# A recommendation tower: twelve bf16-split tables become sixteen float32r-split ones, and the pairs go over DRAM

## The reference

```python
e = jnp.stack([tbl_0[ids[:, 0]], ..., tbl_31[ids[:, 31]]], axis=1)   # 512 x 32 x 128
dot = jnp.einsum('bnd,bmd->bnm', e, e)
iu, ju = jnp.triu_indices(32, k=1)
z = dot[:, iu, ju]                                                  # 512 x 496
h = jnp.concatenate([z, dense_ctx], axis=1)                         # 512 x 512
h = jnp.maximum(h @ W_top1 + b_top1, 0.0)                           # 512 x 512
h = jnp.maximum(h @ W_top2 + b_top2, 0.0)                           # 512 x 256
y = h @ W_top3                                                      # 512 x 1
```

## Time and profile before

| What | us |
|---|---|
| median of 3 runs (lowest to highest) | 162.18 (161.59 to 163.24) |
| the profiled execution, time of the run | 162.2 |
| its span, first to last instruction | 160.4 |
| TensorE busy / VectorE / ScalarE / GpSimd | 135.5 / 86.9 / 51.4 / 80.5 |
| first pick matmul / last table copied / end of the last copy of y | 10.08 / 81.1 / 158.8 |

### The profile page before, as it was taken

The page is one execution under the profiler, slowest core; times in us unless marked ns, Lnnn a source line. Parts: engine busy times, 40 slices in busy tenths (PEclk is TensorE's granted clock), DMA queues, the critical chain, the costliest instruction groups (busy, mean ns, idle before and its releaser), DMA issues.

```text
span 160.4 us, 2998 instructions
## 1 busy us (share of the span) xinstructions
PE 135.5 (84%) x1216; PEld 94.7 (59%) x1222; DVE 86.9 (54%) x218; ACT 51.4 (32%) x124; POOL 80.5 (50%) x88
## 2 busy tenths in 40 slices
PE   0049999999999999999979999799868977647994
PEld 0013454555454455545378998699658966527992
DVE  0299999998898889277029505402741043352010
ACT  3130322440442144123049932001652025462001
POOL 4777777777778777777734773772600000000000
PEclk9999999999999999999999999999999999685699
DMA  3992367646754774989310210220100000000000
GB/s 75 338 356 53 79 235 246 212 115 215 247 145 153 243 223 104 248 315 367 108 48 22 53 49 18 64 54 16 49 20 0 4 0 0 4 0 0 0 0 1
DMA packets 7023, 17.97 MB, mean 112 GB/s; under 512 B 1873, under 2 KB 2513, under 8 KB 6866
## 3 DMA queue, kind: packets, MB, share of 16 engines
q1 hardware_dynamic: 4450, 12.54, 23.5%
q0 software_dynamic: 2560, 5.25, 12.8%
HBM read 17.78 MB, written 0.00 MB: 111 GB/s over the span
## 4 chain that ended last, share of the span: by engine, by line
PE 78%; DVE 9%; ACT 7%; DMA 3%; issue 2%; SPq 1%; DVEq 0%
PE pick_ps L360 41%; PE pick_ps L394 16%; PE dot_ps L382 10%; ACT feat L267 5%; DVE feat L138 4%; DMA table<-picked 3%; PE turn_ps L369 3%; DVE h L208 3%; PE dot_ps L394 2%; PE turn_ps L394 2%; ACT emb L267 1%; PE pick_ps L406 1%; PE pick_ps L433 1%; DVE rest L191 1%; DVE low L194 1%
## 5 line engine op out<-in xcount | busy, mean ns | idle before, releaser
L179 POOL DMA_INDIRECT rows<-tables,row_no x80 | 79.6, 996 | 34.3 <-issue 23.2
L360 PE MATMUL pick_ps<-onehot,table 128*128 128x512 bf16 x97 | 37.7, 389 | 10.2 <-DVE onehot L204 10.1
L360 PE MATMUL pick_ps<-onehot,rest 128*128 128x512 bf16 x96 | 37.4, 390 | 0.1
L360 PE MATMUL pick_ps<-onehot,low 128*128 128x512 bf16 x95 | 36.9, 388 | 0.1
L204 DVE TENSOR_SCALAR onehot<-pick_id,own_row 128x512 bf16<-128x512 f16 x98 | 31.5, 382 | 2.3 <-PE pick_ps L360 2.0
L138 DVE COPY feat<-dot_ps 16x128 f32<-16x128 f32 (+3 forms) x72 | 19.9, 276 | 19.9 <-PE dot_ps L382 19.0
L394 PE MATMUL pick_ps<-feat,w_sb 128*128 128x128 f32 x208 | 26.0, 288 | 4.0 <-ACT feat L267 4.0
L267 ACT ACTIVATE emb<-pick_ps 128x512 f32<-128x512 f32 x12 | 12.9, 1076 | 49.1 <-PE pick_ps L360 49.1
L394 PEld LDWEIGHTS pick_ps<-feat,w_sb 128*128 128x128 f32 x208 | 25.1, 202 | 4.6 <-ACT feat L267 4.3
L360 PEld LDWEIGHTS pick_ps<-onehot,table 128*128 128x128 bf16 x98 | 9.8, 100 | 21.1 <-issue 10.6
L267 ACT ACTIVATE feat<-dot_ps 16x128 f32<-16x128 f32 (+3 forms) x72 | 18.3, 254 | 10.9 <-PE dot_ps L382 10.2
(11 more groups left out here) (32 smaller groups left out, 41.0 us busy)
## 6 DMA issues: line engine op xcount, KB each, us to landing
table<-picked SPq DMA_DIRECT2D x11, 512.0 KB, 3.6
pick_id_sb<-pick_ids SPq DMA_DIRECT2D x12, 256.0 KB, 4.1
w_sb<-w SPq DMA_DIRECT2D x1, 2048.0 KB
rows<-tables,row_no POOLq DMA_INDIRECT x80, 2.8
table<-picked SPq DMA_DIRECT2D x1, 640.0 KB, 7.4
w_sb<-w SPq DMA_DIRECT2D x1, 512.0 KB
feat<-context SPq DMA_DIRECT2D x1, 256.0 KB, 8.5
id_sb<-row_ids SPq DMA_DIRECT2D x1, 80.0 KB, 1.9
```

What stands on the lines that cost most here:

```text
L179: pool.indirect_dma_start(rows[:, k % ROWS_HELD, i, :], None, tables, bass.IndirectOffsetOnAxis(ap=row_no[:, c:c + 1], axis=0)).then_inc(r ...
L360: last = pe.matmul(out, part[:, at, D * k:D * (k + 1)], onehot[:, c % HOT, :], start=(k == 0 and m == 0), stop=(k == KR[t] - 1 and m == le ...
```

## The change

Numbers first: sixteen tables are picked (eleven of 8 chunks, five of 10: 138 chunks), sixteen gathered (64 gathers, 16 turns; twelve turns stand between picks and four between groups of dots). Row buffers are eight.

A picked table has two parts, both of type float32r. ScalarE copies the table into `high` (`split_high`), VectorE subtracts it from the table into `low` (`split_low`), and TensorE makes two matmuls a chunk. The one-hots are float32r too, compared from 16-bit integer ids that are loaded so. The last one-hot of every table is made by ScalarE in two activations, absolute difference and then 1 minus it (`make_last_onehot`). The first table is loaded in four pieces.

The 32 x 32 products are copied to `dot_sb`, four copies a group and engine, and SyncE stores a block of 128 samples to DRAM in four stores, waits, and loads it back in four loads with the row length taken as 33. So partition a gets, for 16 steps k, the product of features a and a+k+1 (modulo 32, shifted by a row where it wraps): each of the 496 pairs once, and the context, which had been stored behind them. W_top1 then has its own 512 rows. `layer1` is 16 matmuls of 256 columns, and there are two halves of 256 samples in place of four blocks. The layers stand behind all dots and turns. The weights are loaded behind the tables and the context, as before, W_top1 in two loads of 512 KB.

```diff
-PICK = 12
+PICK = 16
...
-TABLES_HELD, IDS_HELD, HOT, ROWS_HELD = 3, 4, 12, 6
+TABLES_HELD, IDS_HELD, HOT, ROWS_HELD = 3, 4, 12, 8
+TURN_WITH = [1, 3, 4, 6, 7, 9, 10, 11, 12, 13, 14, 15]
...
+            for r in range(BLOCKS):
+                sp.wait_ge(dots_act, 2 * r + 2)
+                sp.wait_ge(dots_dve, 2 * r + 2)
+                for s in range(4):
+                    sp.dma_start(dot_out[r][s, 0:F * F, :].rearrange("(a j) g -> a (j g)", j=F),
+                                 dot_sb[32 * s:32 * s + 32, r % 2, :, :].rearrange("p j g -> p (j g)")
+                                 ).then_inc(dots_stored[r], 16)
+                sp.wait_ge(dots_stored[r], 64)
+                skewed = dot_out[r].rearrange("s (a x) g -> a s x g", x=F + 1)
+                for q in range(4):
+                    sp.dma_start(pairs[32 * q:32 * q + 32, r, :, :, :].rearrange("a s c g -> a s (c g)"),
+                                 skewed[:, :, 1 + PC * q:1 + PC * (q + 1), :].rearrange("a s c g -> a s (c g)")
+                                 ).then_inc(pairs_in[r], 16)
...
-                dve.tensor_tensor(rest[:, at, 0:n], table[:, at, 0:n], table_hi[:, at, 0:n],
-                                  ALU.subtract).then_inc(rest_ready, 1)
-                dve.wait_ge(rest_ready, t + 1)
-                dve.tensor_tensor(low[:, at, 0:n], rest[:, at, 0:n], rest_hi[:, at, 0:n],
-                                  ALU.subtract).then_inc(low_ready, 1)
+                dve.tensor_tensor(low[:, at, a:b], table[:, at, a:b], high[:, at, a:b],
+                                  ALU.subtract).then_inc(low_ready, 1)
...
+            def make_last_onehot(t):
+                i, k, c = STEPS.index(KR[t]), KR[t] - 1, CHUNK0[t + 1] - 1
+                act.wait_ge(pick_ids_in[t], 16)
...
+                act.activation(away[:, :], pick_id[:, t % IDS_HELD, :], ACT.Abs,
+                               bias=less_row[:, i, k:k + 1]).then_inc(away_ready, 1)
+                act.wait_ge(away_ready, t + 1)
...
+                act.activation(onehot[:, c % HOT, :], away[:, :], ACT.Relu, bias=1.0, scale=-1.0
+                               ).then_inc(last_onehot_ready, 1)
...
             for t in range(PICK):
                 pick_out(t)
+                if t + 1 < PICK:
+                    make_last_onehot(t + 1)
+                if t in TURN_WITH:
+                    emb_out(TURN_WITH.index(t))
                 if t + 3 < PICK:
-                    ids_out(t + 3)
+                    split_high(t + 3)
...
+                    pe.matmul(out, high[:, at, D * k:D * (k + 1)], onehot[:, c % HOT, :],
+                              start=(k == 0), stop=False)
+                    pe.matmul(out, low[:, at, D * k:D * (k + 1)], onehot[:, c % HOT, :],
+                              start=False, stop=(k == KR[t] - 1)).then_inc(picked_done, 1)
...
-            def layer1(r):
-                pe.wait_ge(feat_act, 2 * r + 2)
-                pe.wait_ge(feat_dve, 2 * r + 2)
+            def layer1(v):
+                pe.wait_ge(pairs_in[2 * v], 64)
+                pe.wait_ge(pairs_in[2 * v + 1], 64)
                 for n in range(N1):
...
+                    for c in range(PC):
+                        last = pe.matmul(h1_ps[v][n], w1_sb[:, c, n * P:(n + 1) * P],
+                                         pairs[:, 2 * v:2 * v + 2, :, c, :],
+                                         start=(c == 0), stop=(c == PC - 1))
```

More of the change, by code:

```diff
@@ L36, in build @@
 def build(nc, row_ids, pick_ids, tables, picked, context, w1, w2, small, y):
-    f32, bf16, i32 = mybir.dt.float32, mybir.dt.bfloat16, mybir.dt.int32
-    f16 = mybir.dt.float16
+    f32, f32r, i32, i16 = mybir.dt.float32, mybir.dt.float32r, mybir.dt.int32, mybir.dt.int16
     ALU = mybir.AluOpType
@@ new lines, in _ @@
+            for grp in range(GROUPS):
+                dve.wait_ge(dots, grp + 1)
+                if grp >= 4:
+                    dve.wait_ge(dots_stored[grp // 2 - 2], 64)
+                copy_dots(dve.tensor_copy, grp, (2, 3)).then_inc(dots_dve, 1)
+            for v in range(2):
+                dve.wait_ge(h1_done, 2 * v + 1)
+                for n in (0, 1):
+                    last = relu(h1[:, v, n, :], h1_ps[v][n], b1, n)
+                last.then_inc(h1_dve, 1)
+            for v in range(2):
+                dve.wait_ge(h2_done, 2 * v + 2)
+                relu(h2[:, v, 1, :], h2_ps[v][1], b2, 1).then_inc(h2_dve, 1)
@@ L289, in dots_out @@
-            def dots_out(grp):
-                act.wait_ge(dots, 2 * grp + 2)
-                copy_dots(copy, grp, (0, 1)).then_inc(feat_act, 1)
[L293 to L297, removed]
-            def last_h1_relu(n):
-                act.wait_ge(h1_done, LAST + n + 1)
-                act.activation(h1[:, LAST % 2, n, :], last_h1_ps[n], ACT.Relu,
-                               bias=b1[:, n:n + 1]).then_inc(h1_act, 1)
@@ new lines, in dots_out, with y_out @@
+            def dots_out(grp):
+                act.wait_ge(dots, grp + 1)
+                if grp >= 4:
+                    act.wait_ge(dots_stored[grp // 2 - 2], 64)
+                copy_dots(copy, grp, (0, 1)).then_inc(dots_act, 1)
+            def y_out(v):
+                act.wait_ge(y_done, v + 1)
+                out = y_row[:, HALF * v:HALF * (v + 1)].rearrange("p (r g s) -> p r s g", r=2, s=4)
+                copy(out, y_ps[v].rearrange("p (r s g) -> p r s g", r=2, s=4)).then_inc(y_copied, 1)
@@ L312, in _ @@
+            for j in range(PIECES0):
+                act.wait_ge(piece_in[j], 16)
+                n = PIECE * D
+                copy(high[:, 0, n * j:n * (j + 1)], table[:, 0, n * j:n * (j + 1)]).then_inc(high_ready, 1)
+            make_last_onehot(0)
+            split_high(1)
+            split_high(2)
             for t in range(PICK):
                 pick_out(t)
+                if t + 1 < PICK:
+                    make_last_onehot(t + 1)
+                if t in TURN_WITH:
+                    emb_out(TURN_WITH.index(t))
```

436 lines of the change are left out of this document (184 added, 252 removed).

## The result

| | median, us (runs) | ratio to before, 95% interval |
|---|---|---|
| before, beside it | 161.88 (161.02 to 163.24, 4) | |
| changed kernel | 145.18 (143.57 to 147.14, 4) | 0.893 (0.882 to 0.904) |
| forecast | 131.9 (range 122 to 143) | |

A forecast was written before the change was run, and what follows sets the result against it. TensorE held 78% of the chain; in the changed picks ScalarE would bound tables 1 to 10, TensorE the last five. Dots start at 76.3, the span ends 53.8 later at 130.1, plus 1.8: 131.9 us, range 122 to 143.

The forecast's parts named there:

- GpSimd needs 1.25 a gather ... the 64th begins at 82 undisturbed, say 86: Gathers beside the picks: last one lands by 89, before the last turn at 90.6, so hidden.
- D + 18.5: End of dots: D is when dots start; eight groups at 2.11 and four turns take 18.5 from there.
- Float32r matmul: Picks on TensorE: 0.216 per 512-column matmul, the bf16 pace; 59.6 in all, 3.9 less than before.
- Rival B: Picks on TensorE: float32r matmuls run at half pace, 0.43 to 0.46 each; time 187 to 197; chance 0.08.
- VectorE in the picks: One-hots keep 0.329 each and one subtraction is left: a table takes 3.55, or 4.45 with 10 chunks.
- Rival A: Picks on VectorE: 4-byte one-hots make one element a cycle, 0.58 each, bounding the picks; time 153.6; chance 0.12.
- ScalarE in the picks: Copies, last one-hots and splits: 3.75 an iteration, 4.4 with a turn, so ScalarE bounds tables 1 to 10.
- D = 76.3: End of the picks: dots start at 76.3, against 81.1 before.
- The way over DRAM: Pairs stored and reloaded by SyncE: 5.9 a block, bounding this stage; store lands in 2.5, loads in 2.2.
- Rival C: Pairs over DRAM: a store takes 5 us to land, second half's pairs come 10 later; time 142; chance 0.10.
- the forecast's ladder: After dots start (D): layer 1 at D + 19.6, its second half at D + 31.4, span ends at D + 53.8.
- 2 to spare: Last gather, landing by 89, against the last turn at 90.6: the forecast margin before gathers delay TensorE.

The follow-up runs named there:

- f3b: Changed kernel with float16 table parts and one-hots, each subtraction in 4 or 5 instructions, and a new order of the end layers: 128.41 us, ratio 0.798.
- f4: Changed kernel with float16 table parts and one-hots and each subtraction in 4 or 5 instructions, its own end order kept: 129.98 us, ratio 0.808.
- a1b: Changed kernel with VectorE's one-hots written as bf16 beside, TensorE reading one standing float32r one-hot (picked rows wrong): 133.0 us, one execution.
- f1: Changed kernel with both table parts and all one-hots in float16 (table scaled by 256), same number of matmuls: 131.07 us, ratio 0.814.

## Why the prediction was wrong

**The step that failed** is the gathers' pace: "GpSimd needs 1.25 a gather ... the 64th begins at 82 undisturbed, say 86". Nearly undisturbed that is right (f3b and f4, mean 0.990, last at 84.7 and 84.8). In the changed kernel it is 1.32 + 0.3 in the mean, and the last begins at 105.8. The prediction left VectorE out of this price, though it gave VectorE a new form of one-hot. From there the sum is short: dots end at 115.4 instead of D + 18.5 = 94.8, so 20.6 late, and the end after them takes 27.7 instead of 35.3, 7.6 less, for while TensorE waited for rows SyncE's queue caught up with stores and loads. With the gathers out of the way the end came near its price: 33.6 in a1b, 33.5 in f4. 20.6 - 7.6 = 13.0, the whole difference of the spans (143.1 to 130.1).

**How the wrong price came about.** I read from the earlier trace rows that the gather keeps 0.95 beside one-hots and took the mean of eight, 0.329, for a one-hot's price. The same stretch instruction by instruction, VectorE and the gather:

```profile
24.86 0.34 DVE L204 TENSOR_SCALAR onehot<-pick_id,own_row 128x512 bf16<-128x512 f16 x1
25.13 0.55 DVE L204 TENSOR_SCALAR onehot<-pick_id,own_row 128x512 bf16<-128x512 f16 x1
25.60 0.33 DVE L204 TENSOR_SCALAR onehot<-pick_id,own_row 128x512 bf16<-128x512 f16 x1
```

```profile
24.62 0.95 POOL L179 DMA_INDIRECT rows<-tables,row_no  x1 [0.30 <-issue]
```

One-hots begin 0.27 apart, but the one of 25.13 took 0.55: it ended at 25.68, 0.11 after the gather's end at 25.57. All 19 one-hots of that kernel that took over 0.45 ended so, 0.11 to 0.12 after a gather. The two engines did exclude each other before; there the one-hot waited, once a gather, and the mean hid it. The subtractions could be seen to hold gathers there too: eight gathers between 38 and 73 took 1.06 to 1.74, and each touched one; the earlier trace rows was taken where none did. Free of that a 16-bit one-hot is 0.262 and a 4-byte one 0.397. Both fit 0.13 and 1.05 ns a cycle, with 128 cycles and with 256 for the 512 elements, so four and two elements a cycle; 1.05 ns an element is the slope of the changed kernel's subtractions, (1.480 - 1.211)/256. So the row of the Trainium skill that I quoted (VectorE: DVE Perf Modes, The perf-mode tier table: four in bf16, two in float32) holds in this trace, and my "the trace has two" was wrong. Had I believed the row, the next step was to ask which ports such a mode takes.

Point by point:
- **Start**: first matmul at 6.2 (forecast 5.3), table 1 done near 12.1 (11.1). The ids were there at 4.85, not 4.3, and then two one-hots of 0.40 and a subtraction of 0.42 took 1.3, not 1.0.
- **Float32r matmul**: 0.228 apart beside weight loads of 0.200 (0.216 with loads of 0.100 for float16). Rival B is out. 276 x 0.012 is 3.3 us. The Trainium skill's 614 GB/s for TensorE's moving operand (SBUF — State Buffer, A bandwidth-pool intuition that's wrong) doesn't bound it: 128 x 512 x 4 bytes in 0.228 are 1150 GB/s.
- **VectorE in the picks**: a one-hot 0.397, not 0.329; a table cycle 3.91, not 3.55. Rival A's one element a cycle (0.58) did not come, but its suspicion, that the 4-byte output changes what the one-hots share with GpSimd, was the right one, with the wrong victim.
- **ScalarE in the picks**: forecast as the bound with 3.75 and 4.4. It bounds nothing: in the changed kernel, a1b, f3b and f4 it waits for TensorE in nearly every iteration, TensorE never waits over 0.1 for its last one-hot, and its own work is 3.2 and 3.7, for its instructions overlap by some 0.1 where I added handovers. TensorE bounds the picks: iterations of 3.65 and 4.09 with a turn in a1b, 3.45 and 3.89 in f3b, which are its 16 matmuls and the turn. VectorE's 3.91 in the changed kernel is about the mean of 3.65 and 4.09, and three of the first eight iterations are 0.1 to 0.3 longer there. ScalarE's price, 0.5 to 0.7 too long, made up for the late start and the longer matmuls.
- **D = 76.3**: 90.4 in the changed kernel, where two turns among the picks waited for rows; 78.4 in a1b, 75.1 in f4. Near, and in part by luck, as the bullet before says.
- **The way over DRAM**: landings 2.2 (store) and 2.1 (loads) against 2.5 and 2.2, copies 0.42 (VectorE) and 0.37 (ScalarE) against 0.43; Rival C is out. With gathers out of the way the forecast's ladder stands: in f4 layer 1 begins at D + 21.4 (forecast D + 19.6), its second half at D + 32.5 (D + 31.4), the span ends at D + 51.6 (D + 53.8).
- **TensorE idle before the second half and half clock behind it**: not in the changed kernel (1.44, then 7.14, full pace). In a1b it came so, 3.41 and then 8.83; forecast were over 4 and 9.7. In f4 the longer idle, 3.21, was before the first half, and that half took 8.83.

```profile
110.35 8.83 PE L419 MATMUL dot_ps<-pairs,w_sb 128*128 128x256 f32 x32 [3.41 <-DMA pairs<-dot_out]
```

The cause is shown, not only argued: remove the 4-byte one-hots alone and the time is 133.0, against 131.9 forecast, and f1, which makes two-byte one-hots and leaves nothing out, takes 131.07. The sizing of everything else was near, partly because errors cancelled. Open is why a 16-bit one-hot gives way to a gather while a 4-byte one doesn't, though by the rates above both use more than one element a cycle.

## What to carry to other kernels

Where GpSimd issues indirect DMAs beside VectorE, price both together: one-hots with a 4-byte output, and subtractions with two SBUF inputs, lengthened many of the gathers that ran beside them, and gathers issued back to back all through the kernel have no slack to take it. Split a merged row into its instructions before you call its mean a price: a mean of 0.329 was five times 0.26, once 0.32 and twice 0.47 from one start to the next. Look for the stretch where the thing you price is disturbed, not only for one where it isn't. And when you take a resource with "2 to spare", work out what it does if each of its items becomes a third longer.

## What the runs showed of the hardware

- VectorE and GpSimd's indirect DMAs hold each other up in both directions. The loser ends mostly 0.11 to 0.12 after an end of the winner's. 16-bit one-hots lose to a gather (0.55 in place of 0.34); 4-byte one-hots, and subtractions of 1024 or 1280 columns, win over it (1.2 to 5.1 in place of 0.94, up to 2.1 with 16-bit one-hots beside).
- A hold may last past the ends of ten instructions (3.81) and of thirteen (4.94). Splitting the subtractions cured most of it with two-byte one-hots (excess 9.8 to 3.0) and none with 4-byte ones (27.7 and 32.4).
- Two-input subtractions alone hold gathers (excess 0.9 without, 8.3 with them), though they make one element a cycle.
- A float32r matmul of 512 columns costs 0.228 where bf16 and float16 cost 0.216; its weights load in 0.200 against 0.100.
